# Expert layer of a two-layer decoder: slots inverted by one-hot products, rows gathered and results scattered inside the experts' stage, gate folded into a token-major projection

## The chip, the cores and the metric

One core of one Trainium2 chip runs the whole program. The metric is the device time of one execution in microseconds (us); lower is better. The core's engines are TensorE (PE), VectorE (DVE), ScalarE (ACT), GpSimd (POOL) and SyncE (SP), which here only issues DMAs. Each engine runs its own list of instructions in order and waits on semaphores; an instruction that waits holds up all that stand behind it on the same engine.

## The reference, cut to what matters

The program is two decoder layers on x of 2 x 1024 tokens by 256. The change is in the last block, a mixture of 8 experts of which each token takes 2:

```python
h = x @ W_in + b_in                       # x: after layernorm, 2048 x 256
t = h.reshape(B * S, -1)
logits = t @ W_gate + b_gate              # 2048 x 8
probs = jax.nn.softmax(logits, axis=-1)
topv, topi = jax.lax.top_k(probs, TOP_K)  # TOP_K = 2
topv = topv / jnp.sum(topv, axis=-1, keepdims=True)
route = jnp.zeros_like(probs).at[jnp.arange(t.shape[0])[:, None], topi].set(topv)
mid = jax.nn.relu(jnp.einsum('nd,edh->neh', t, W1) + b1)    # W1: 8 x 256 x 1024
eout = jnp.einsum('neh,ehd->ned', mid, W2) + b2             # W2: 8 x 1024 x 256
moe_out = jnp.einsum('ne,ned->nd', route, eout)
out = moe_out.reshape(B, S, -1) @ W_out + b_out             # added to x
```

## The kernel before, in words

`x` stays in SBUF as 16 blocks (`NT`) of 128 tokens (`P`). The expert layer is three programs one after the other, each ended by a barrier of all engines.

`moe_prepare`: LayerNorm in 4 groups of 4 blocks; PE transposes to `mp_xt`; the projection with W_in gives `mp_full` with the features on the partitions (L1827); the gate (`Route.tensor`, L919) multiplies `mp_full` by W_gate, 128x8 at a time; PE transposes `mp_full` back (L1839) and ACT copies it to `mp_token`. DVE picks two experts per token and `Places.vector` computes a slot number for each choice: the choices are sorted by expert, and each expert's list is padded to a multiple of 256 rows (`RT`). That makes 23 tiles (`TILES`) of 256 slots, each with one expert. POOL first fills `moe_rows` in DRAM with zeros through `mp_zeros` (L1806, L1796), and then scatters each block of tokens twice by indirect DMA, 32 in all (L1813).

`moe_experts`: a loop over the 23 tiles. SP loads the tile's 256 rows into `me_row` (2 buffers), its biases, and the expert's W1 and W2 in 4 chunks of 512 KB (`me_chunk`, 4 buffers). ACT and DVE split each chunk into a high and a low part (`me_w_parts`, L2023 and L2058), the rows likewise (`take`, `me_h`), so that each product is three fp32r products. PE's order is written out by hand: `first(u+1)`, then `turn(u+2)` (the transposition of the rows of tile u+2), then `second(u)`. `first` makes the 8 blocks of the middle layer (L1983), ACT and DVE turn each into `me_mid` (L2045, L2047, L2086), `second` makes the result (L1997), and DVE's `finish(u - 2)` adds b2 into `me_result` (L2075) after the fifth block of tile u:

```python
for u in range(TILES):
    for b in range(HB):
...
        if b == HB - 1 and u + 1 < TILES:
            take(u + 1)
...
        if b == 4 and u >= 2:
            finish(u - 2)
```

POOL stores each result tile as it lies (L1957).

`moe_collect`: for each block of 128 tokens POOL gathers the two result rows of each token by indirect DMA (L2135, 32 in all, 4 buffers); DVE scales and adds them (L2186, L2188), PE transposes (L2146) and multiplies by W_out (L2158), DVE adds to `x` (L2179). Then `x` is stored.

## Time and profile before

| | us |
|---|---|
| median of 3 runs | 1904.73 (1901.89 to 1906.77) |
| the profiled execution's own time | 1912.87 |
| its span | 1911.2 |
| PE busy in the span | 1438.0 (75%) |
| DVE busy | 1089.6 (57%) |
| ACT busy | 898.0 (47%) |
| POOL busy | 308.2 (16%) |

The span is the time from the first to the last instruction of the profiled execution; starts of instructions are counted from its beginning. Busy shares are averages over stages of different kinds. The expert layer begins at 1423.2 us.

### The profile page before, as it was taken

The page shows a single profiled execution, that of the slowest core. Times are in us where ns is not written, and L with a number is a line of the kernel's source. Part 1 is how long each engine was busy: PE and PEld are TensorE (multiplying, and loading weights), DVE is VectorE, ACT ScalarE, POOL GpSimd, SP SyncE. Part 2 cuts the span into 40 slices and gives each one's busy share as a digit, 9 for nine tenths or more (in the row PEclk, how much of TensorE's full clock was granted, in tenths as well). Part 3 has the DMA queues.
Part 4 walks back from the last instruction along what each step waited for, and adds up shares of the span by engine and source line. Part 5 has one row for each costly group of instructions (what it writes and reads, how often), then busy time and mean ns, then how long its engine had stood idle before and what let it go on. Part 6 is the DMA issues. An engine that isn't in the chain of part 4 may idle for free. (4 is left out here: it accounts for less than half of the span.)

```text
span 1911.2 us, 28538 instructions
## 1 busy us (share of the span) xinstructions
PE 1438.0 (75%) x10307; PEld 1073.4 (56%) x10307; DVE 1089.6 (57%) x2450; ACT 898.0 (47%) x2137; POOL 308.2 (16%) x338
## 2 busy tenths in 40 slices
PE   4758889988589999789981453588868059999964
PEld 2413333334379999656760231477755059999953
DVE  3657766741655555455668647456553047777753
ACT  1503555553256666331104775366542057887731
POOL 1200000002223333200001525100010600000034
PEclk8858999998799999979995665799887579999987
DMA  2371322200200000110000000211112256766623
GB/s 68 132 99 20 49 35 35 35 2 9 81 1 2 1 1 2 34 39 1 0 23 9 1 6 14 64 35 34 34 47 88 88 188 219 222 216 217 227 85 103
DMA packets 92688, 122.59 MB, mean 64 GB/s; under 512 B 22221, under 2 KB 74051, under 8 KB 92291
## 3 DMA queue, kind: packets, MB, share of 16 engines
q1 hardware_dynamic: 86675, 105.85, 20.5%
q0 software_dynamic: 4912, 14.42, 2.1%
q8 instruction: 83, 1.36, 0.3%
q10 hardware_dynamic: 960, 0.47, 0.1%
q14 instruction: 58, 0.48, 0.1%
HBM read 88.60 MB, written 24.67 MB: 59 GB/s over the span
## 5 line engine op out<-in xcount | busy, mean ns | idle before, releaser
L759 DVE TENSOR_REDUCE sa_top<-ps 128x1 f32<-128x512 f32 (+3 forms) x384 | 197.2, 553 | 96.3 <-PE ps L751 65.3
L787 ACT ACTIVATE sa_probs<-ps 128x1024 f32<-128x1024 f32 (+4 forms) x192 | 150.8, 811 | 204.1 <-PE ps L772 145.6
L751 PE MATMUL ps<-sa_k,sa_q 96*128 96x512 bf16 (+3 forms) x384 | 125.5, 365 | 55.5 <-DMA sa_k<-scr_k 28.5
L1983 PE MATMUL ps<-me_h,me_w_parts 128*128 128x256 f32 x1104 | 142.0, 289 | 14.5 <-DVE me_w_parts L2058 7.9
L1983 PEld LDWEIGHTS ps<-me_h,me_w_parts 128*128 128x128 f32 x1104 | 136.8, 192 | 18.7 <-issue 15.3
L1997 PE MATMUL ps<-me_w_parts,me_mid 128*128 128x256 f32 x1104 | 136.2, 283 | 6.1 <-DVE me_result L2075 6.1
L1997 PEld LDWEIGHTS ps<-me_w_parts,me_mid 128*128 128x128 f32 x1104 | 132.3, 188 | 10.5 <-issue 10.5
L2735 ACT ACTIVATE cx_p<-ps,cx_top 128x154 f32<-128x154 f32 x256 | 97.2, 389 | 86.4 <-DVE cx_top L2799 86.4
L751 PEld LDWEIGHTS ps<-sa_k,sa_q 96*128 96x128 bf16 x384 | 35.1, 98 | 160.7 <-DVE sa_top L759 89.1
L2058 DVE TENSOR_TENSOR me_w_parts<-me_chunk,me_w_parts 128x1024 fp32r<-128x1024 f32 x92 | 112.8, 1226 | 21.4 <-ACT me_w_parts L2023 18.6
L2045 ACT ACTIVATE me_full<-ps,me_b 128x256 f32<-128x256 f32 x184 | 95.0, 517 | 57.6 <-PE ps L1983 54.5
L2086 DVE TENSOR_TENSOR me_mid<-me_full,me_mid 128x256 fp32r<-128x256 f32 x184 | 76.9, 422 | 65.8 <-ACT me_mid L2047 65.8
L772 PE MATMUL ps<-sa_q,sa_k 99*128 99x512 bf16 (+3 forms) x384 | 108.2, 335 | 7.6 <-ACT sa_probs L787 7.5
L2023 ACT ACTIVATE me_w_parts<-me_chunk 128x1024 fp32r<-128x1024 f32 x92 | 104.6, 1137 | 3.8 <-DMA me_chunk<-in_L_ffn_W_dram 3.8
L3164 ACT ACTIVATE cn_p<-ps,cn_top 128x154 f32<-128x154 f32 x256 | 82.1, 397 | 43.7 <-DVE cn_top L3248 43.5
L2047 ACT ACTIVATE me_mid<-ps,me_b 128x256 fp32r<-128x256 f32 x184 | 96.2, 523 | 0.0
L2597 POOL TENSOR_TENSOR cx_pn<-cx_p,cx_rinv 128x512 f32<-128x512 f32 x64 | 66.8, 1043 | 171.3 <-DVE cx_rinv L2807 171.2
L1058 PE MATMUL ps<-f_w_high,f_hid 128*128 128x512 f32 (+1 forms) x320 | 91.9, 373 | 0.0
L796 PE MATMUL ps<-sa_probs,v_all 128*32 128x512 f32 (+3 forms) x768 | 76.9, 503 | 0.0
L850 POOL TENSOR_TENSOR x<-x,po_b 128x256 f32<-128x256 f32 x16 | 11.0, 727 | 361.8 <-DMA po_w<-in_L_attn_Wout_dram 361.8
L772 PEld LDWEIGHTS ps<-sa_q,sa_k 99*128 99x128 bf16 x384 | 38.0, 100 | 49.5 <-ACT sa_probs L787 16.9
L1957 POOL DMA_DIRECT2D moe_results<-me_result x23 | 16.6, 720 | 301.1 <-DVE me_result L2075 301.1
(397 smaller groups left out, 3530.7 us busy)
## 6 DMA issues: line engine op xcount, KB each, us to landing
me_chunk<-in_L_ffn_W_dram SPq DMA_DIRECT2D x92, 512.0 KB, 5.4
sa_q<-scr_q SPq DMA_DIRECT2D x48, 128.0 KB, 4.8
sa_k<-scr_k SPq DMA_DIRECT2D x48, 128.0 KB, 7.7
moe_rows<-mp_zeros SPq DMA_DIRECT2D x2, 2944.0 KB, 12.7
me_row<-moe_rows SPq DMA_DIRECT2D x23, 256.0 KB, 3.8
moe_results<-me_result POOLq DMA_DIRECT2D x23, 256.0 KB, 3.2
cn_qd<-cn_qh SPq DMA_DIRECT2D x64, 64.0 KB, 2.0
scr_q<-h_part SPq DMA_DIRECT2D x6, 512.0 KB, 3.9
```

The lines of the kernel that those rows point to most:

```text
L751: last = pe.matmul(c.ps[:, bank, 0:w], self.q_st[0:96, slot, h, P * sb:P * sb + P], self.k_st[0:96, slot, h, k0:k0 + w], start=True, stop= ...
L759: return dve.tensor_reduce(self.top2[:, k0 // 512, ST * h + sb:ST * h + sb + 1], self.c.ps[:, bank, 0:w], AX.X, ALU.max)
L772: last = pe.matmul(out[:, 0:qw], self.k_st[0:KROWS, slot, h, P * kb:P * kb + P], self.q_st[0:KROWS, slot, h, P * kb + q0:P * kb + q0 + qw] ...
L787: return act.activation(dst, src, ACT.Exp, scale=self.width ** -0.5)
L1058: last = pe.matmul(ps[:, 4 + n % 4, 0:w], hid[:, g % 2, net, m, part, cols], wt[:, m, w0:w0 + w], start=(i == 0), stop=(i == len(terms) - 1))
L1983: last = pe.matmul(ps[:, MID + n % 4, 0:RT], w[:, u % 2, 0, i, DM * k + P * b:DM * k + P * b + P], h[:, u % 2, j, k, :], start=(m == 0), s ...
L1997: last = pe.matmul(ps[:, OUT + n % 2, 0:D], mid[:, u % 2, b, i, P * a:P * a + P], w[:, u % 2, 1, j, D * b:D * b + D], start=(m == 0), stop ...
L2023: act.activation(part(n, 0), chunk[:, n % BUF, :], ACT.Copy).then_inc(w_high.sem, 1)
L2045: act.activation(full[:, n % 4, :], ps[:, MID + n % 4, 0:RT], ACT.Relu, bias=col).then_inc(s_full.sem, 1)
L2047: act.activation(mid[:, u % 2, b, 0, :], ps[:, MID + n % 4, 0:RT], ACT.Relu, bias=col).then_inc(high.sem, 1)
L2058: dve.tensor_tensor(part(n, 1), chunk[:, n % BUF, :], raw(part(n, 0)), ALU.subtract).then_inc(w_low.sem, 1)
L2735: last = act.activation(p[:, h + i, :], ps[:, S_BANK + n % SR, M * i:M * i + M], ACT.Exp, bias=top[:, t % 2, h + i:h + i + 1], accum_out=d ...
```

## The change

The three programs become two. `moe_prepare`, `Places` and the use of `Route` and `LayerNorm` go; a class `Prepare` runs at the head of `moe_experts` instead, without a barrier between it and the experts. In it:

- PE first forms W_in @ W_gate and sets it beside W_in (`WL` = 264 columns). The projection is then one product with the tokens on the partitions, whose last 8 columns are the logits. It starts while LayerNorm of later groups still runs, and ACT takes half of LayerNorm's blocks.
- The tokens are stored to DRAM in their own order (`moe_tokens`, 4 plain DMAs on SP); the zero fill and the 32 scatters go.
- The slot numbers are inverted: with a slot = 128 a + b, DVE builds one-hot rows of a (`one_a`) and of b (`one_b`), POOL multiplies one of them by the list number (`pool_scale`), and 32 PE products of 92 columns give for each slot which token stands there. From that DVE forms `source` (the row to read) and `target` (where the result goes).
- In the experts' loop POOL gathers a tile's rows by `source` (two indirect DMAs of 128 rows), scatters its results by `target` to where the tokens' two results lie in order (two more), and adds b_out to one block of `x` in each of the first 16 tiles. SP's loop loses the row load and orders the weights ahead of the biases.
- `moe_collect` loads all results with 8 plain DMAs of 512 KB, 4 on SP and 4 on ACT. ACT takes one of the two scalings from DVE. W_out and b_out are loaded at the start of `Prepare`.

The diff, cut to its core:

```diff
+        for m in range(KD):
+            last = pe.matmul(ps[:, 5, E8 * KD:E8 * KD + E8], self.b_cols[:, m, :], self.w_gate[:, m, :],
+                             start=(m == 0), stop=(m == KD - 1))
+        last.then_inc(self.s["gate_made"].sem, 1)
+        turn(1)
+        pe.wait_ge(self.s["gate_set"].sem, self.s["gate_set"].at(2))
+        for g in range(NG):
+            hidden(g)
+            if g + 2 < NG:
+                turn(g + 2)
...
+        for i in range(LISTS):
+            if i % 8 == 0:
+                pe.wait_ge(self.s["hot_b"].sem, self.s["hot_b"].at(i // 8 + 1))
+            if i == 0:
+                pe.wait_ge(self.s["scaled"].sem, self.s["scaled"].at(2))
+            last = pe.matmul(ps[:, self.LIST, 0:2 * SLOTS], self.one_b[:, i, :],
+                             self.named[:, i, :, :].rearrange("p a s -> p (a s)"), start=(i == 0), stop=(i == LISTS - 1))
+        last.then_inc(self.s["listed"].sem, 1)
...
+        reverse = self.rev[:, :].unsqueeze(1).to_broadcast([P, NT, E8])
+        for j, src in enumerate((logits, self.rest[:, :, :])):
+            then(dve.tensor_reduce(self.top[:, j, :], src, AX.X, ALU.max))
+            then(dve.tensor_tensor(self.same[:, :, :], src, spread(self.top[:, j, :]), ALU.is_equal))
+            then(dve.tensor_tensor(self.scored[:, :, :], self.same[:, :, :], reverse, ALU.mult))
+            then(dve.tensor_reduce(self.rank[:, j, :], self.scored[:, :, :], AX.X, ALU.max))
+            then(dve.tensor_tensor(self.pick[:, j, :, :], self.scored[:, :, :], spread(self.rank[:, j, :]), ALU.is_equal))
+            if j == 0:
+                then(dve.scalar_tensor_tensor(self.rest[:, :, :], self.pick[:, 0, :, :], FAR, logits, ALU.mult, ALU.add))
+        dve.tensor_tensor(self.gone[:, 0, :], self.top[:, 1, :], self.top[:, 0, :], ALU.subtract).then_inc(self.s["gap"].sem, 1)
...
+        dve.tensor_tensor(self.one_a[:, :, :], self.iota_a[:, :].unsqueeze(1).to_broadcast([P, LISTS, SLOTS]),
+                          self.slot_a[:, :].unsqueeze(2).to_broadcast([P, LISTS, SLOTS]), ALU.is_equal
+                          ).then_inc(self.s["hot_a"].sem, 1)
+        dve.wait_ge(self.s["hot_a"].sem, self.s["hot_a"].at(1))
+        dve.tensor_scalar(self.named[:, :, 0, :], self.one_a[:, :, :], self.col[:, :], None, ALU.mult
+                          ).then_inc(self.s["scaled"].sem, 1)
...
+        for q in range(LISTS // 8):
+            a = slice(8 * q, 8 * q + 8)
+            dve.tensor_tensor(self.one_b[:, a, :], self.iota_b[:, :].unsqueeze(1).to_broadcast([P, 8, P]),
+                              self.slot_b[:, a].unsqueeze(2).to_broadcast([P, 8, P]), ALU.is_equal
+                              ).then_inc(self.s["hot_b"].sem, 1)
+        dve.wait_ge(self.s["listed"].sem, self.s["listed"].at(1))
+        then(dve.tensor_copy(self.found[:, :, :].rearrange("p a s -> p (a s)"), ps[:, self.LIST, 0:2 * SLOTS]))
+        then(dve.scalar_tensor_tensor(self.value[:, :], self.found[:, 1, :], float(P), self.found[:, 0, :],
+                                      ALU.mult, ALU.add))
+        then(dve.tensor_scalar(self.late[:, :], self.value[:, :], N + 0.5, -float(N), ALU.is_ge, ALU.mult))
+        then(dve.scalar_tensor_tensor(self.late[:, :], self.late[:, :], -1.0, self.value[:, :], ALU.add, ALU.add))
+        dve.tensor_scalar(self.source[:, :], self.late[:, :], 0.0, None, ALU.max).then_inc(self.s["sourced"].sem, 1)
...
-                sp.wait_ge(zero.sem, zero.at(1))
-                for i in range(ZERO):
-                    sp.dma_start(rows[P * per * i:P * per * (i + 1), :].rearrange("(p r) d -> p (r d)", p=P),
-                                 zeros[:, :]).then_inc(zeroed.sem, 16)
-                sp.wait_ge(bset.sem, bset.at(1))
...
-                pool.memset(zeros[:, :], 0.0).then_inc(zero.sem, 1)
-                places.pool(pool)
-                pool.wait_ge(zeroed.sem, zeroed.at(16 * ZERO))
-                pool.wait_ge(places.placed.sem, places.placed.at(1))
-                for t in range(NT):
-                    pool.wait_ge(tset.sem, tset.at(t + 1))
-                    for j in range(TK):
-                        pool.indirect_dma_start(rows, bass.IndirectOffsetOnAxis(ap=place[:, t, j:j + 1], axis=0),
-                                                token[:, t, :], None).then_inc(sent.sem, 16)
-                pool.wait_ge(sent.sem, sent.at(16 * NT * TK))
...
-                route.tensor(pe, full, w_gate)
-                for t in range(NT):
-                    if t >= 8 and t % 2 == 0:
-                        pe.wait_ge(tset.sem, tset.at(t - 6))
-                    for k in range(KD):
-                        last = pe.transpose(ps[:, t // 2 % 4, D * (t % 2) + P * k:D * (t % 2) + P * k + P],
-                                            full[:, k, P * t:P * t + P], c.ident[:, :])
...
             def _(sp):
+                pr.sync_loads(sp, w_out, b_out)
+                pr.sync_stores(sp, tokens, b1_cols)
                 for u in range(TILES):
...
-                    if u >= 2:
-                        sp.wait_ge(turned.sem, turned.at(u - 1))
-                    sp.dma_start(row[:, u % 2, :, :], rows[RT * u:RT * u + RT, :].rearrange("(a p) d -> p a d", p=P)
-                                 ).then_inc(row_in[u % 2].sem, 16)
...
+                    e = sp.value_load(pr.expert[0:1, u:u + 1], min_val=0, max_val=E8 - 1)
+                    def weights(q):
...
+                    weights(0)
+                    weights(1)
...
+                def gather(u):
+                    if u >= 2:
+                        pool.wait_ge(turned.sem, turned.at(u - 1))
+                    for a in range(SUB):
+                        at = bass.IndirectOffsetOnAxis(ap=pr.source[:, SUB * u + a:SUB * u + a + 1], axis=0)
+                        pool.indirect_dma_start(row[:, u % 2, a, :], None, tokens, at).then_inc(row_in[u % 2].sem, 16)
+                def scatter(u):
+                    pool.wait_ge(added.sem, added.at(SUB * (u + 1)))
+                    for a in range(SUB):
+                        at = bass.IndirectOffsetOnAxis(ap=pr.target[:, SUB * u + a:SUB * u + a + 1], axis=0)
+                        pool.indirect_dma_start(results, at, result[:, u % 2, a, :], None).then_inc(stored[u % 2].sem, 16)
...
+                gather(0)
+                gather(1)
+                pool.wait_ge(pr.s["targeted"].sem, pr.s["targeted"].at(1))
                 for u in range(TILES):
-                    pool.wait_ge(added.sem, added.at(SUB * (u + 1)))
-                    pool.dma_start(results[RT * u:RT * u + RT, :].rearrange("(a p) d -> p a d", p=P),
-                                   result[:, u % 2, :, :]).then_inc(stored[u % 2].sem, 16)
+                    if u < NT:
+                        pool.tensor_tensor(c.x[:, u, :], c.x[:, u, :], b_out[:, :], ALU.add).then_inc(biased.sem, 1)
+                    if u + 2 < TILES:
+                        gather(u + 2)
+                    scatter(u)
+                pool.wait_ge(biased.sem, biased.at(NT))
                 for i in range(2):
-                    pool.wait_ge(stored[i].sem, stored[i].at(16 * len(range(i, TILES, 2))))
...
+        def load(eng, j):
+            for g in range(NG):
+                r0 = N * j + 4 * P * g
+                eng.dma_start(got[:, j, 4 * g:4 * g + 4, :],
+                              results[r0:r0 + 4 * P, :].rearrange("(t p) d -> p t d", p=P)).then_inc(got_in[j][g].sem, 16)
...
-                sp.dma_start(bb[:, :], c.arg["L1_ffn_b_out"].rearrange("(a b) -> a b", a=1).partition_broadcast(P)
-                             ).then_inc(w_in.sem, 16)
-                sp.dma_start(w[:, :, :], c.arg["L1_ffn_W_out"].rearrange("(k p) n -> p k n", p=P)
-                             ).then_inc(w_in.sem, 16)
...
-            def _(pool):
-                for t in range(NT):
-                    if t >= RING:
-                        pool.wait_ge(summed.sem, summed.at(t - RING + 1))
-                    for j in range(TK):
-                        pool.indirect_dma_start(got[:, t % RING, j, :], None, results,
-                                                bass.IndirectOffsetOnAxis(ap=place[:, t, j:j + 1], axis=0)
-                                                ).then_inc(got_in[t % RING].sem, 16)
+                load(sp, 0)
...
+                load(act, 1)
+                def weigh(t):
+                    act.wait_ge(got_in[0][t // 4].sem, got_in[0][t // 4].at(16))
+                    if t >= 2:
+                        act.wait_ge(summed.sem, summed.at(t - 1))
+                    act.activation(part[:, t % 2, :], got[:, 0, t, :], ACT.Copy, scale=share[:, 0, t:t + 1]
+                                   ).then_inc(weighed.sem, 1)
+                weigh(0)
+                weigh(1)
...
-                dve.wait_ge(w_in.sem, w_in.at(32))
-                for t in range(NT):
-                    dve.tensor_tensor(c.x[:, t, :], c.x[:, t, :], bb[:, :], ALU.add).then_inc(biased.sem, 1)
...
-                    dve.wait_ge(got_in[t % RING].sem, got_in[t % RING].at(16 * TK * (t // RING + 1)))
+                    dve.wait_ge(got_in[1][t // 4].sem, got_in[1][t // 4].at(16))
+                    dve.wait_ge(weighed.sem, weighed.at(t + 1))
                     if t >= 2:
                         dve.wait_ge(turned.sem, turned.at(t - 1))
-                    m, g = mixed[:, t % 2, :], got[:, t % RING, :, :]
-                    dve.tensor_scalar(m, g[:, 0, :], share[:, t, 0:1], None, ALU.mult).then_inc(weighed.sem, 1)
-                    dve.wait_ge(weighed.sem, weighed.at(t + 1))
-                    dve.scalar_tensor_tensor(m, g[:, 1, :], share[:, t, 1:2], m, ALU.mult, ALU.add
-                                             ).then_inc(summed.sem, 1)
+                    dve.scalar_tensor_tensor(mixed[:, t % 2, :], got[:, 1, t, :], share[:, 1, t:t + 1], part[:, t % 2, :],
+                                             ALU.mult, ALU.add).then_inc(summed.sem, 1)
```

POOL's instructions in the experts' loop, in the order before. `[waits signal49]` is here `added`, DVE's count of finished result halves.

```order
L1953 UNCONDITIONAL_BRANCH [waits barrier_Pool_Activation_PE_DVE_SP_gather]
L1957 DMA moe_results<-me_result 128x2x256 [waits signal49] x23
L1922 UNCONDITIONAL_BRANCH [waits me_stored1,me_stored0]
```

The same place after. `signal54` is `added`, `signal44` is `turned` (PE's count of transposed row tiles); the first four gathers are those of tiles 0 and 1.

```order
L2072 DMA me_row<-moe_tokens,mp_source 128x256 [waits signal31,signal21]
L2072 DMA me_row<-moe_tokens,mp_source 128x256 x3
L2088 TENSOR_TENSOR x<-x,moe_b_out 128x256 [waits signal32]
L2072 DMA me_row<-moe_tokens,mp_source 128x256 [waits signal44]
L2072 DMA me_row<-moe_tokens,mp_source 128x256
L2078 DMA moe_results<-me_result,mp_target 9984x256 [waits signal54]
L2078 DMA moe_results<-me_result,mp_target 9984x256
L2088 TENSOR_TENSOR x<-x,moe_b_out 128x256
L2072 DMA me_row<-moe_tokens,mp_source 128x256 [waits signal44]
L2072 DMA me_row<-moe_tokens,mp_source 128x256
L2078 DMA moe_results<-me_result,mp_target 9984x256 [waits signal54]
L2078 DMA moe_results<-me_result,mp_target 9984x256
```

A stage that was one plain DMA a tile is now an add, two gathers and two scatters; the gathers of tile 3 stand behind the scatters of tile 0, and so on.

PE after, from the last block of `first(2)` to `second(1)` and `first(3)`. `me_row_in1` is the landing of the gathers of tile 3.

```order
L2117 MATMUL ps<-me_h,me_w_parts 128x256 [waits signal51]
L2117 MATMUL ps<-me_h,me_w_parts 128x256 x5
L2104 MATMUL ps<-ident,me_row 128x128 [waits signal46,me_row_in1]
L2104 MATMUL ps<-ident,me_row 128x128 x3
L2131 MATMUL ps<-me_w_parts,me_mid 128x256 [waits signal54,signal52,signal48]
L2131 MATMUL ps<-me_w_parts,me_mid 128x256 x23
L2131 MATMUL ps<-me_w_parts,me_mid 128x256 [waits signal54]
L2131 MATMUL ps<-me_w_parts,me_mid 128x256 x23
L2117 MATMUL ps<-me_h,me_w_parts 128x256 [waits signal51,signal48,signal46]
L2117 MATMUL ps<-me_h,me_w_parts 128x256 x5
```

PE's order within the experts' loop is as before; what the transposition waits for has moved from SP's load to POOL's gathers.

## Rows read from the trace of the kernel before

**Rows 1.** Timeline, preparation: start us, duration us, engine, line, operation, count [idle before].

```profile
1423.17 5.01 POOL L1806 MEMSET mp_zeros<- 128x5888 f32 x1 [60.17 <-POOLq L2933]
...
1424.93 3.42 DVE L180 TENSOR_SCALAR lnm_ve<-lnm_mv 128x4 f32<-128x4 f32 x1
...
1441.22 13.95 PE L1827 MATMUL ps<-mp_xt,mp_w 128*128 128x512 f32 x32
...
1455.95 12.26 PE L919 MATMUL ps<-mp_gate,mp_full 128*128 128x8 f32 x64 [0.78 <-ACT mp_full L1851]
...
1468.24 0.29 DVE L933 TENSOR_TENSOR rt_logits<-ps,rt_bias 128x128 f32<-128x128 f32 x1 [26.59 <-PE ps L919]
...
1542.77 7.48 PE L1983 MATMUL ps<-me_h,me_w_parts 128*128 128x256 f32 x47 [7.93 <-DVE me_w_parts L2058]
```

**Rows 2.** Busy time by stretch: PE, PEld, DVE, ACT, POOL, granted clock, DMA share, GB/s.

```profile
1484.00:1531.00 47.00, 0.00 (x0) 0.00 (x0) 1.15 (x5) 0.00 (x0) 31.09 (x32) 0.50 0.22 89
...
1545.00:1830.00 285.00, 272.48 (x2192) 264.33 (x2190) 204.37 (x334) 230.49 (x475) 14.42 (x20) 0.99 0.65 209
...
1552.00:1556.00 4.00, 0.00 (x0) 0.00 (x0) 3.88 (x6) 3.58 (x7) 0.00 (x0) 0.66 0.63 212
...
1857.00:1903.00 46.00, 29.00 (x96) 20.21 (x96) 18.46 (x48) 6.14 (x16) 24.36 (x25) 0.70 0.26 75
```

**Rows 3.** Indirect DMAs by tile, time on POOL: min/median/max ns, first and last start.

```profile
L1813 POOL DMA_INDIRECT moe_rows<-mp_token,moe_place x32: 959/963/1244, 1485.0 to 1524.6; - x32
...
L2135 POOL DMA_INDIRECT mc_got<-moe_results,moe_place x32: 946/949/1170, 1848.1 to 1892.2; - x32
```

**Rows 4.** Timeline, one tile of the experts.

```profile
1810.79 6.06 PE L1983 MATMUL ps<-me_h,me_w_parts 128*128 128x256 f32 x48
1811.83 0.47 ACT L2045 ACTIVATE me_full<-ps,me_b 128x256 f32<-128x256 f32 x1 [2.40 <-PE ps L1983]
...
1816.68 0.60 PE L1970 MATMUL ps<-ident,me_row 128*128 128x128 f32 x4
...
1816.98 0.75 DVE L2075 TENSOR_TENSOR me_result<-ps,me_b 128x256 f32<-128x256 f32 x2
...
1817.55 5.93 PE L1997 MATMUL ps<-me_w_parts,me_mid 128*128 128x256 f32 x48 [0.27 <-DVE me_result L2075]
...
1818.03 0.72 POOL L1957 DMA_DIRECT2D moe_results<-me_result  x1 [11.91 <-DVE me_result L2075]
...
1822.09 1.23 DVE L2058 TENSOR_TENSOR me_w_parts<-me_chunk,me_w_parts 128x1024 fp32r<-128x1024 f32 x1
1823.42 6.05 PE L1983 MATMUL ps<-me_h,me_w_parts 128*128 128x256 f32 x48
```

**Rows 5.** Costliest groups: an add of 256 elements on POOL.

```profile
L850 POOL TENSOR_TENSOR x<-x,po_b 128x256 f32<-128x256 f32 x16 | 11.0, 727 | 361.8 <-DMA po_w<-in_L_attn_Wout_dram 361.8
```

**Rows 6.** DMA issues: count, KB each, median us from issue to landing.

```profile
me_chunk<-in_L_ffn_W_dram SPq DMA_DIRECT2D x92, 512.0 KB, 5.4
...
me_row<-moe_rows SPq DMA_DIRECT2D x23, 256.0 KB, 3.8
```

**Rows 7.** Timeline, collection.

```profile
1847.44 0.35 SPq L2124 DMA_DIRECT2D mc_b<-in_L_ffn_b_out_dram  x1
...
1873.37 0.42 DVE L2179 TENSOR_TENSOR x<-ps,x 128x256 f32<-128x256 f32 x1 [6.50 <-remote]
...
1884.22 0.95 POOL L2135 DMA_INDIRECT mc_got<-moe_results,moe_place  x1 [0.30 <-issue]
...
1887.67 0.34 DVE L2186 TENSOR_SCALAR mc_mixed<-mc_got,moe_share 128x256 f32<-128x256 f32 x1
...
1901.88 0.43 DVE L2179 TENSOR_TENSOR x<-ps,x 128x256 f32<-128x256 f32 x1 [1.01 <-PE ps L2158]
```

**Rows 8.** Timeline of PE alone, the second tile of the experts.

```profile
1556.93 7.37 PE L1983 MATMUL ps<-me_h,me_w_parts 128*128 128x256 f32 x48 [6.13 <-issue]
```

532 lines of the change are left out of this document (309 added, 223 removed).

## The prediction

> **What bounds the kernel now.** I read the table of stages first, then the timeline of each stage. The change touches only the last 488 us of the span, the second layer's expert part, and that part is four stretches with four different bounds.
>
> Preparation, 1423.2 to 1484. LayerNorm, projection, gate and a transposition follow each other. [rows 1] show the projection's matmuls at 13.95 us and then the gate's 64 at 12.26 us, with VectorE (DVE) idle until the logits are complete at 1468.24; the slot numbers are complete just before the first scatter at 1485.0 [rows 3]. At the front a 5.01 us memset on GpSimd (POOL) runs beside a DVE instruction on 4 values a partition that lasts 3.42 us, so DVE waits there.
>
> Scatter, 1484 to 1531. [rows 2] put no TensorE (PE) work at all there: POOL builds 32 indirect DMAs. Each is 0.96 us of POOL [rows 3], 1.27 us from start to start (1485.0 to 1524.6 over 31 steps). PE's first expert matmul comes at 1542.77 [rows 1].
>
> Experts, 1545 to 1830. PE is busy 272.5 of 285 us at a granted clock of 0.99 [rows 2]. One tile in [rows 4]: `first` starts at 1810.79 and at 1823.42, so a tile takes 12.63 us. Between them stand the transposition of the next rows (1816.68), which does not wait, and `second` (1817.55). DVE finishes the results of the tile two before at 1816.98 to 1817.73, and POOL sends them at 1818.03, after 11.91 us idle. POOL is idle nearly all the time, which decides nothing by itself.
>
> Collection, 1847.4 to 1902.3. 32 gathers at 0.95 us plus 0.30 us on POOL [rows 3] set the pace; PE is busy 29 of 46 us at clock 0.70 [rows 2].
>
> **The change part by part.** *Preparation and scatter.* The projection keeps its columns (32 matmuls of 264 in place of 16 of 512), but begins while LayerNorm runs, and brings the logits with it: 12.26 us of gate go. Eight loads instead of seven stand before PE, W_out among them, and two bias chains; I give back 2 us. So logits at about 1458. Then DVE's chain. From logits to the first scatter it took 16.8 us; now it has 11 operations for the two choices (0.32 each, by the 0.29 us row at 1468.24 and its gap), 1.3 for the counts, 1.2 through PE, 2.0 to `expert`, 3.0 to `slot_b`. The one-hot rows are new and have no row: `one_a` has 1472 elements and `one_b` four times 1024. The nearest row, a DVE operation on 1024 elements, takes 1.23 us [rows 4], so 1.8, 1.7 and 4.9 us; POOL's product of 1472 elements costs 4.2 us by its 0.73 us for 256 [rows 5] and lies beside them. With 1.9 for the last matmuls and the decoding it is 21 us: `source` at 1479. Two gathers (0.3 + 2.5), landing 2.5, transposition and two halves of `me_h` 2.6: first expert matmul at 1487 in place of 1542.77, **-56 us**. Weights load from `expert` (about 1466) on, beside all this. If the new broadcasts ran at half the element rate it is -45; if LayerNorm gains in full from the missing memset, -64.
>
> *Collection.* Eight plain loads of 512 KB on two queues replace the gathers. The nearest row, weights of 512 KB, lands in 5.4 us [rows 6], so the first product starts about 6 us after 1847.44. DVE loses 16 adds and 16 scalings. PE then has 1.8 us a token block at clock 0.70 (29.0/16), so about 1.3 at the full one: 3 blocks at 2.1 and 13 at 1.3, with a tail of 2, end 31 us after 1847.44 and not 54.9 [rows 7]: -24. But DVE stood 6.50 us there for a releaser that the trace does not know [rows 7], and such a stop would no longer hide behind POOL: I take **-20**, with -10 and -26 as bounds. The last tile's scatter is two indirect DMAs instead of one plain, **+2**.
>
> *Experts.* SyncE (SP) loses the row load, POOL gets two gathers, two scatters and one add a tile: 4 x 1.27 + 0.93, about 6.0 us of 12.6. By sum that fits. The order does not. POOL issues gather(u+3) behind scatter(u), and scatter(u) waits at POOL's head until `finish(u)` is done. DVE does `finish(u)` after the fifth `me_mid` of tile u+2, which needs `first(u+2)` on PE. And PE wants the rows of tile u+3 directly after `first(u+2)`. So gather(u+3) starts only when its rows are already due, for every u from 0 to 19: 20 tiles. The old row load on SP waited only for the transposition two tiles before. Behind PE's late transposition stand `second`, the next `first`, and ScalarE's (ACT) and DVE's `take`, then their splits.
>
> The period follows from [rows 4]. From the start of `first` to the end of `finish`: 1817.73 - 1810.79 = 6.94. ACT is idle 2.40 us before its first copy there, so it brings no backlog and this number stays. Then POOL: 0.30 to wake (1818.03 - 1817.73), two scatters 2.52, add 0.73 [rows 5] and 0.20, two gathers 2.20 up to the end of the second's building: 5.95. Landing has no row of its own. Above: a gather built at 1885.17 was read at 1887.67 at the latest, 2.5 [rows 7]; the plain row load took 3.8 beside the weights [rows 6]. Below I put 1.5 (that row load less its issue and queueing, an estimate). I take 2.5. Then the transposition and `second` up to the next `first`, 0.60 + 5.87. Sum 21.86. PE stands 9 us before that; after 6.13 us idle, in which the granted clock fell (0.66 on average over its end) [rows 2], 48 matmuls took 7.37 instead of 6.05 [rows 4, 8]: +1.4. Period **23.3**, 10.6 more than 12.63. The add is there in 15 of the 20 cases: 15 x 10.6 + 5 x 9.7 = **+208 us**. Lower bound, landing 1.5, no clock loss, no gap at the add: 8.0, in all +156. Upper, landing 3.8, four builds at 1.17 [rows 3], clock loss doubled: 14.3, in all +282.
>
> Sum: 208 - 56 - 20 + 2 = **+134 us**. The profiled execution took 1912.87 around a span of 1911.2, 8 us above the median 1904.73; all terms are differences, so I put them on the median: **2039 us** (2047 on the profiled one).
>
> **A page that bears on it.** In the trace, gathers took up to 1.17 us of POOL where 0.95 is the median [rows 3]. The Trainium skill, in "SBUF — State Buffer", section "SBUF: two separate sides", says of DMAs issued from GpSimd that their descriptors can't be written while DVE holds the shared port in a two-port mode, and gives 620 ns growing to 3100. The trace agrees in direction only, with a tenth or two in place of five times. What it would do here is the second rival.
>
> **The rivals.** *Faster, 7 in 100: the rows are not late.* If POOL's building overlapped its waits, or gathers cost it nothing, the tile would stay at 12.63 and the gains stay: 1904.7 - 74 = **1831**. For it: POOL idle 11.91 us a tile, and six more fit. Against: the order above, and indirect DMAs that follow each other at a fixed 1.27 us, never overlapping. It decides for faster from where finish-to-rows-landed takes under 16.3 - 6.94 - 6.47 = 2.9 us (74 us over 20 tiles allow 3.7 each); two scatters alone take 2.5.
>
> *Slower still, 8 in 100: the building waits for DVE.* If each of the four in the late chain waits for one of DVE's 1.23 us subtractions, 4.9 us a tile, +98: **2137**. For it the 1.17; against it that DVE stands at `take` when the gathers are built.
>
> *The clock, 3 in 100.* If pauses of 9 us keep PE at its lower level (1.2 GHz) through `second` and half of `first`, some 8 us a tile more: about **2180**. Against: 48 matmuls after 6.13 us idle lost only 1.3 us.
>
> *Preparation gains nothing, 4 in 100:* small operations and waits eat the gain of the gate and the scatter: 2039 + 56 less some, about **2085**.
>
> **How the numbers follow.** The forecast has 78 in 100. Its terms' bounds, all at once, give 1972 (156 - 64 - 26 + 1 = +67) and 2134 (282 - 45 - 10 + 2 = +229); the ends of all terms rarely meet, and with the rivals above it the range that leaves out 2 in 10 is 1985 to 2110. A change of 0.3% (about 6 us) is what a measurement of this kernel can tell from none. Slower: all but the first rival, 0.93. Within 0.3%: only if the late chain is close to 2.9 us, 0.01. Faster 0.06.
>
> **What would show it.** In the profile after: POOL's `me_row` gathers start within 5 us after DVE's `me_result`, and PE's transposition of `me_row` is preceded by 7 to 11 us idle in every tile from the fourth on, with the clock low after it; starts of `first` 21 to 25 us apart; experts about 500 us long in all; first expert matmul 50 to 60 us earlier; collection 25 to 35 us instead of 55. POOL busy share small all the same. Wrong would be: a tile period near 13 us, gathers that start before `me_result`, or a preparation as long as before.

## The result, and the profile after

The changed kernel takes 2066.0 us (median of 4 runs, 2065.5 to 2073.6) against 1904.5 us (4 runs, 1901.9 to 1906.8): ratio 1.086, 95% interval 1.083 to 1.088. The forecast was 2039 us in a range of 1985 to 2110. The profiled execution has a span of 2064.4 us; the one of before had 1911.2 us.

The page of the profile, two lines of its table of 40 slices (busy tenths of PE, and tenths of its granted clock). The experts fill slices 30 to 39. PE is at 5 and 6 there, once at 7, with the clock at 7 and 8; in the kernel before, whose line stands behind them, the experts' slices show 9:

```profile
PE   4569988876799997999246248886465566555574
...
PEclk9859999988899997899655569998787778887787
...
PE   4758889988589999789981453588868059999964
```

The chain of waits, 1500 to 1980 us (waiting line, releaser: us in total, times, longest):

```profile
POOL moe_results L2078 <- DVE me_result L2211: 355.7, 19, 34.4
...
PE ps L2104 <- DMA me_row<-moe_tokens,mp_source: 196.5, 19, 11.6
```

In the kernel before, PE's transposition of a tile's rows had no wait at all [rows 4]. Now it waits 10.3 us on average in each of the 19 tiles of this window, for the gather. One tile on the timeline of the changed kernel, to be read against [rows 4]:

```profile
1753.73 5.98 PE L2117 MATMUL ps<-me_h,me_w_parts 128*128 128x256 f32 x48
...
1759.86 0.75 DVE L2211 TENSOR_TENSOR me_result<-ps,me_b 128x256 f32<-128x256 f32 x2
...
1760.88 1.00 POOL L2078 DMA_INDIRECT moe_results<-me_result,mp_target  x1 [17.46 <-DVE me_result L2211]
...
1762.19 1.01 POOL L2078 DMA_INDIRECT moe_results<-me_result,mp_target  x1 [0.30 <-issue]
...
1762.79 1.58 DVE L2194 TENSOR_TENSOR me_w_parts<-me_chunk,me_w_parts 128x1024 fp32r<-128x1024 f32 x1
...
1763.22 1.73 POOL L2088 TENSOR_TENSOR x<-x,moe_b_out 128x256 f32<-128x256 f32 x1
...
1765.11 0.99 POOL L2072 DMA_INDIRECT me_row<-moe_tokens,mp_source  x1 [0.16 <-issue]
1766.40 0.96 POOL L2072 DMA_INDIRECT me_row<-moe_tokens,mp_source  x1 [0.30 <-issue]
1769.79 1.12 PE L2104 MATMUL ps<-ident,me_row 128*128 128x128 f32 x4 [10.08 <-DMA me_row<-moe_tokens,mp_source]
...
1770.56 7.23 PE L2131 MATMUL ps<-me_w_parts,me_mid 128*128 128x256 f32 x48
```

The reader is to follow one chain down the list: result finished at 1760.61, two scatters, addition, two gathers built by 1767.36, rows read at 1769.79, second product, and the next first product at 1777.62. PE's transposition and second product are slower than in [rows 4] and come later, and each step of this chain stands behind the one before it.

The stages, each read from the same points in both traces:

| stretch | before | after | difference |
|---|---|---|---|
| start of the expert layer to first expert matmul | 119.6 | 67.7 | -51.9 |
| first expert matmul to the end of the last second product | 299.1 | 531.0 | +232.0 |
| from there to the first load or gather of the collection | 5.6 | 12.5 | +6.9 |
| from there to the last addition of the collection | 54.9 | 26.5 | -28.4 |

The sum is +158.6 us. The profiled execution reached the expert layer 4.8 us earlier (1418.4 and not 1423.2), ahead of anything the change touches, and its tail was 0.7 us shorter; that leaves the 153.2 us between the spans.

The end of the preparation, to be read against [rows 1] and [rows 3]:

```profile
1467.58 3.00 POOL L1752 TENSOR_TENSOR mp_xt<-mp_one_a,mp_list 128x1472 bf16<-128x1472 bf16 x1 [46.48 <-DVE mp_one_a L1952]
...
1467.98 7.08 DVE L1960 TENSOR_TENSOR mp_xt<-mp_iota_b,mp_slot_b 128x1024 bf16<-128x1024 f32 x4
...
1478.03 1.21 POOL L2072 DMA_INDIRECT me_row<-moe_tokens,mp_source  x1 [7.45 <-DVE mp_source L1969]
...
1486.13 7.73 PE L2117 MATMUL ps<-me_h,me_w_parts 128*128 128x256 f32 x48 [1.41 <-DVE me_h L2199]
```

The end of the experts and the start of the collection, to be read against [rows 7]:

```profile
2017.22 0.42 DVE L2211 TENSOR_TENSOR me_result<-ps,me_b 128x256 f32<-128x256 f32 x1 [2.32 <-PE ps L2131]
...
2019.20 0.97 POOL L2078 DMA_INDIRECT moe_results<-me_result,mp_target  x1 [0.30 <-issue]
2029.66 2.29 SPq L2258 DMA_DIRECT2D mc_got<-moe_results  x4
```

Two things stand out that the prediction had not. The tile periods are not all alike: the first 15 take 23.9 us on average (1514.43 to 1873.30), the last five, which have no addition on POOL, 25.1 us (1873.30 to 1998.73) and not less. And from the last scatter to the first load 9.5 us pass in which no engine computes.

### The profile page after: what moved, and what is told of

Same layout as the page of the kernel before. It is cut to its first block and busy times, and to the rows that moved or that the text cites. A ratio compares the mean times of both kernels' runs of the same rounds, so it can differ in the third digit from the quotient of the medians.

```text
span 2064.4 us, 28469 instructions
## 1 busy us (share of the span) xinstructions
PE 1446.0 (70%) x10291; PEld 1094.0 (53%) x10291; DVE 1102.5 (53%) x2396; ACT 903.2 (44%) x2142; POOL 347.6 (17%) x366
## 5 line engine op out<-in xcount | busy, mean ns | idle before, releaser
L2104 PE MATMUL ps<-ident,me_row 128*128 128x128 f32 x92 | 24.6, 419 | 214.1 <-DMA me_row<-moe_tokens,mp_source 214.1
L2131 PE MATMUL ps<-me_w_parts,me_mid 128*128 128x256 f32 x1104 | 163.7, 317 | 0.9 <-DVE me_result L2211 0.9
L2131 PEld LDWEIGHTS ps<-me_w_parts,me_mid 128*128 128x128 f32 x1104 | 160.5, 225 | 1.0 <-issue 1.0
L2223 DVE TENSOR_TENSOR me_mid<-me_full,me_mid 128x256 fp32r<-128x256 f32 x184 | 84.6, 464 | 141.4 <-ACT me_mid L2183 141.4
L2104 PEld LDWEIGHTS ps<-ident,me_row 128*128 128x128 f32 x92 | 15.9, 210 | 218.4 <-DMA me_row<-moe_tokens,mp_source 218.4
L2194 DVE TENSOR_TENSOR me_w_parts<-me_chunk,me_w_parts 128x1024 fp32r<-128x1024 f32 x92 | 117.6, 1279 | 22.5 <-ACT me_w_parts L2158 19.9
L2078 POOL DMA_INDIRECT moe_results<-me_result,mp_target x46 | 46.6, 1013 | 410.0 <-DVE me_result L2211 403.0
L2199 DVE TENSOR_TENSOR me_h<-ps,me_h 128x512 fp32r<-128x512 f32 x23 | 15.9, 691 | 140.9 <-ACT me_h L2164 140.9
```

What stands on the lines that cost most here:

```text
L2131: last = pe.matmul(ps[:, OUT + n % 2, 0:D], mid[:, u % 2, b, i, P * a:P * a + P], w[:, u % 2, 1, j, D * b:D * b + D], start=(m == 0), stop ...
L2194: dve.tensor_tensor(part(n, 1), chunk[:, n % BUF, :], raw(part(n, 0)), ALU.subtract).then_inc(w_low.sem, 1)
```

## The experiments

The theory: gather(u+3) stands on POOL behind scatter(u), which waits for a result that exists only when the rows of u+3 are due. The rivals: indirect transfers are slow in themselves; POOL and DVE disturb each other; PE's clock. All times below are medians; the kernel before was timed beside each, at 1905.8 to 1908.1 us, and the ratios are to it.

### The gather ahead of the wait

```diff
+                gather(2)
                 for u in range(TILES):
+                    if u + 3 < TILES:
+                        gather(u + 3)
                     if u < NT: pool.tensor_tensor(...)
-                    if u + 2 < TILES:
-                        gather(u + 2)
                     scatter(u)
```

> Edit: on POOL the row gather of tile u+3 is issued ahead of the addition and of the wait for tile u's result, instead of behind the scatters of tile u; nothing else differs from the changed kernel. Theory (the rows arrive late because the gathers stand behind the scatter's wait for the result): the rows are there when TensorE asks, a tile takes about 12.6 to 13.5 us again instead of 24.2, 20 tiles give back 20 x (24.2 - 13) = 224 us, and 2066 - 224 = about 1840 us. Rival A (the indirect transfers themselves are too slow beside the weight loads, whatever their place): the wait for the rows stays, the period stays at 22 us or more, 2020 us or more. Rival B (POOL's and VectorE's collisions take over as the bound): a period of 15 to 18 us, 1880 to 1940 us.

Measured: 1837.9 us, ratio 0.963 (0.960 to 0.966). The transfers and the additions are the same, the gathers stand elsewhere in POOL's list, and the kernel takes 228 us less than the changed one. Two neighbouring tiles on its timeline:

```profile
1604.72 6.04 PE L2118 MATMUL ps<-me_h,me_w_parts 128*128 128x256 f32 x48
...
1610.98 0.66 PE L2105 MATMUL ps<-ident,me_row 128*128 128x128 f32 x4 [0.22 <-DMA me_row<-moe_tokens,mp_source]
1611.47 5.94 PE L2132 MATMUL ps<-me_w_parts,me_mid 128*128 128x256 f32 x48
1611.94 1.01 POOL L2078 DMA_INDIRECT moe_results<-me_result,mp_target  x1 [5.71 <-DVE me_result L2212]
...
1614.55 1.37 POOL L2072 DMA_INDIRECT me_row<-moe_tokens,mp_source  x1 [0.30 <-issue]
...
1616.00 1.23 DVE L2195 TENSOR_TENSOR me_w_parts<-me_chunk,me_w_parts 128x1024 fp32r<-128x1024 f32 x1
1616.23 1.84 POOL L2072 DMA_INDIRECT me_row<-moe_tokens,mp_source  x1 [0.31 <-issue]
1617.33 6.05 PE L2118 MATMUL ps<-me_h,me_w_parts 128*128 128x256 f32 x48
```

The period is 12.61 us, that of before; the transposition waits 0.22 us. Over 20 tiles it is 12.65 against 24.21 on average: 231 us. Rivals A and B fall. Rival B's collisions are there: a gather takes 1.37 and 1.84 us of POOL instead of 0.96 (mean over the 46: 1.49), but POOL still idles 5.7 us a tile and the period does not grow.

### The order alone, in the kernel before

```diff
-                    sp.dma_start(row[:, u % 2, :, :], rows[...])       # SyncE, ahead of the weights
+                    if u + 2 < TILES:                                  # POOL, behind the store of u - 1
+                        load(u + 2)
```

> Edit of the kernel before: the plain load of a tile's rows moves from SyncE's queue to POOL's, where it stands behind the store of the tile's result, in the order of the changed kernel; no indirect transfer is added to it. Theory (the order on POOL's queue makes the stall): the period goes from 12.63 us to about 20 us (first product to result 6.9, store issue, landing of 4 to 5 us, transposition and second product 6.5), 20 x 7.5 = +150 us, about 2055 us. Rival (the indirect transfers make it, the order alone costs nothing): within 15 us of 1905 us.

Here `load(0)` and `load(1)` stand ahead of the loop, and `load(u + 2)` at its head, so that it follows the store of u - 1 as the gather does. Measured: 2057.6 us, +150 us, ratio 1.080 (1.075 to 1.085). One tile:

```profile
1956.19 0.75 DVE L2079 TENSOR_TENSOR me_result<-ps,me_b 128x256 f32<-128x256 f32 x2
1957.23 0.72 POOL L1961 DMA_DIRECT2D moe_results<-me_result  x1 [18.91 <-DVE me_result L2079]
1957.95 0.71 POOL L1953 DMA_DIRECT2D me_row<-moe_rows  x1
1962.25 1.12 PE L1974 MATMUL ps<-ident,me_row 128*128 128x128 f32 x4 [6.22 <-DMA me_row<-moe_rows]
1963.02 7.90 PE L2001 MATMUL ps<-me_w_parts,me_mid 128*128 128x256 f32 x48
```

With no scatter, no gather and no addition in the stage, the period is 20.1 us. So the order alone costs 7.5 of the 11.6 us that a tile lost. The other 4.1 are a difference of two kernels, not the price of one thing: in the two tiles shown, POOL needs 6.8 us from the result to the second gather where it needs 1.7 here to the end of the load's issue, and the rows land 2.4 us behind that where they take 3.6 here.

### The addition out of the chain

```diff
-                    if u < NT: pool.tensor_tensor(...)
                     if u + 2 < TILES:
                         gather(u + 2)
+                    if u < NT: pool.tensor_tensor(...)
                     scatter(u)
```

> Edit: on POOL the bias addition of a tile stands behind the two gathers instead of ahead of them, all 16 additions stay. Theory (the addition, 1.73 us, and the gap of 0.2 us behind it lie on the late chain of result, scatters, addition, gathers, rows, transpositions, second product, result): 1.9 us less in each of 15 tiles, -28 us, about 2038 us. Rival (the arrival of the rows is set by the weight loads that are under way, as in the last five tiles, where the gathers were built 1.2 us earlier and the rows landed 2.8 us later): the rows land no earlier, 2060 to 2100 us.

Measured: 2065.8 us, ratio 1.083 (1.079 to 1.086). No change; the rival that the rows land no earlier stands, and the step of my working that priced this addition at its own duration falls. On its timeline:

```profile
1760.22 1.01 POOL L2078 DMA_INDIRECT moe_results<-me_result,mp_target  x1 [17.70 <-DVE me_result L2211]
...
1762.84 1.37 POOL L2072 DMA_INDIRECT me_row<-moe_tokens,mp_source  x1 [0.30 <-issue]
...
1764.51 0.97 POOL L2072 DMA_INDIRECT me_row<-moe_tokens,mp_source  x1 [0.30 <-issue]
1765.48 0.75 POOL L2090 TENSOR_TENSOR x<-x,moe_b_out 128x256 f32<-128x256 f32 x1
1769.24 1.11 PE L2104 MATMUL ps<-ident,me_row 128*128 128x128 f32 x4 [10.19 <-DMA me_row<-moe_tokens,mp_source]
```

The result was finished at 1759.94. From there the gathers are built in 5.5 us instead of 6.8, but the rows are read after 9.3 us in the one and 9.2 in the other: they land 3.8 us behind the gathers, not 2.4. Of the addition's 1.9 us, 0.4 went into a longer first gather and the rest into the transfer.

The run says something of the last five tiles too. Here POOL's chain from result to gathers is the same in all twenty tiles, yet the last five take 25.1 us each (1872.58 to 1998.05) and the fifteen before them 23.9, as in the changed kernel. So the longer period of the last five does not come from the missing addition. What it comes from no run shows.

### What holds the rows up in the transfer

Two kernels, both edits of the last one.

```diff
+                        if n >= BUF:           # half of every weight load, q < 2; likewise for q >= 2
+                            src, dst = src[:, 0:DM // 2], dst[:, 0:DM // 2]
                         sp.dma_start(dst, src).then_inc(w_in[n % BUF].sem, 16)
```

> Edit of e2_add_behind: from the second expert tile on each of the four weight loads of a tile fetches half of its bytes (256 KB instead of 512 KB; the other half of the buffer keeps old weights, so the outputs are not the reference's); every instruction on the engines stays. Theory (the rows' transfer takes 3.8 us behind the second gather instead of 2.4 because the weight loads keep the DMA engines at 70 to 90% while it runs): the rows land about 2.4 us behind the second gather, 1.4 us less in each of 20 tiles and a little more where the first gather shrinks from 1.37 to 1.0 us, -28 to -36 us, about 2034 us. Rival (the rows wait for the scatters that stand ahead of them in POOL's queue, 6.7 us from the second scatter's end to the transposition in both orders): within 8 us of 2066 us.

```diff
                 def scatter(u):
                     pool.wait_ge(added.sem, added.at(SUB * (u + 1)))
+                    if u + 3 < TILES:
+                        gather(u + 3)
                     for a in range(SUB): ...
```

> Edit of e2_add_behind: POOL still waits for tile u's result, but then issues the two gathers of tile u+3 first and the two scatters of tile u behind them. Theory (what makes a tile late is the whole chain from result to rows, of which the two scatters' 2.6 us of issue are a part, and the transfer then meets the weight loads wherever it is): the gathers are built 2.6 us earlier, of which some is lost again in the transfer, as the addition's 1.9 us was; the period falls by 0.5 to 2.6 us, -10 to -52 us, 2015 to 2055 us. Rival (the rows are held up by the scatters' transfers ahead of them in the queue): the rows land 2.4 us behind the second gather, 6.3 us after the result instead of 9.3, the period falls by 3 us or more, 2005 us or less. Rival (the weight loads set the arrival alone): no change, 2066 us.

Measured: 2050.9 us (1.077, 1.073 to 1.081) with half the weight bytes, and 2006.4 us (1.052, 1.049 to 1.055) with the gathers ahead of the scatters. A tile of the first:

```profile
1758.38 0.96 POOL L2077 DMA_INDIRECT me_row<-moe_tokens,mp_source  x1 [0.30 <-issue]
...
1761.82 1.11 PE L2109 MATMUL ps<-ident,me_row 128*128 128x128 f32 x4 [8.89 <-DMA me_row<-moe_tokens,mp_source]
```

Its second product, at 1762.58, takes 7.96 us. The rows land 2.5 us behind the second gather (1759.34 to 1761.82; 2.9 in the next tile) instead of 3.8, as the theory said, while the period falls only from 24.21 to 23.37 us. The wait shrinks by 1.2 us, from 10.2 (194.2 us in 19 times) to 9.1 (181.3 in 20), and the second product grows by 0.3, from 7.2 to 7.5 on average (172.1 us over 23 tiles against 166.0). So weight traffic delays the rows by about 1.3 us a tile; the total missed the expected range (-15 us against -28 to -36), since the first gather did not shrink (1.37 us, as before) and the second product gave some back.

And a tile of the second:

```profile
1769.20 0.98 POOL L2072 DMA_INDIRECT me_row<-moe_tokens,mp_source  x1 [16.44 <-DVE me_result L2212]
1770.49 1.01 POOL L2072 DMA_INDIRECT me_row<-moe_tokens,mp_source  x1 [0.30 <-issue]
1771.80 1.41 POOL L2080 DMA_INDIRECT moe_results<-me_result,mp_target  x1 [0.30 <-issue]
...
1775.01 1.11 PE L2105 MATMUL ps<-ident,me_row 128*128 128x128 f32 x4 [6.99 <-DMA me_row<-moe_tokens,mp_source]
```

The period is 21.19 us, 3.0 less than 24.21: more than the scatters' 2.6 us of issue. The total lies below the range of the theory (2015 to 2055 us) and within 2 us of what the first rival had, by which the scatters' own transfers hold the rows up (2005 us or less). Its figure for the rows, 6.3 us behind the result, is nearly met as well (6.1: 1768.93 to 1775.01). Its other figure is not: the rows land 3.5 us behind the second gather here and 4.6 in the tile before, not 2.4. So that rival is neither confirmed nor excluded; the second one, by which the weights set the arrival alone, had no change and falls. What is shown: 2.6 us earlier in the queue brought 3.0 us a tile, 1.9 us earlier brought nothing, and weight traffic takes part. Why the one gain came through and the other did not stays open, since no run here moved the weight loads in time alone.

### TensorE's clock

```diff
                 def turn(u):
-                    pe.wait_ge(row_in[u % 2].sem, ...)
                     if u >= 2:
                         pe.wait_ge(h_low.sem, h_low.at(u - 1))
+                    if u >= 3:
+                        for _ in range(21):
+                            pe.matmul(ps[:, TURN[u % 2], 0:WL], c.ident[:, :], pr.w[:, 0, :], start=True, stop=True)
+                    pe.wait_ge(row_in[u % 2].sem, ...)
```

> Edit: ahead of the wait for a tile's rows TensorE runs 21 products of no use (identity by a 264-column constant, into the bank that the transposition then overwrites), about 9 us of work in a wait of 10 us; they keep the granted clock up and leave the outputs alone. Theory (1.2 to 1.9 us of the period is TensorE's clock falling in the wait: second product 7.23 us instead of 5.93, transposition 1.12 instead of 0.60): -1.7 x 20 = -34 us, about 2032 us. Rival (the second product is slow for another reason than the idle time ahead of it, or the filler delays the transposition by what it wins): within 10 us of 2066 us, or slower.

Measured: 2039.4 us, -26.7 us, ratio 1.069 (1.066 to 1.073).

```profile
1757.13 0.66 PE L2107 MATMUL ps<-ident,me_row 128*128 128x128 f32 x4 [0.48 <-DMA me_row<-moe_tokens,mp_source]
1757.55 5.94 PE L2134 MATMUL ps<-me_w_parts,me_mid 128*128 128x256 f32 x48
```

With PE busy ahead of them, transposition and second product take 0.66 and 5.94 us, as in [rows 4]; in the changed kernel they took 1.12 and 7.23. Windows over the tile of the changed kernel show its clock (us, busy PE, PEld, DVE, ACT, POOL; PEclk, DMA share, GB/s): 0.67 over the wait, 0.58 over the first 4 us of work behind it, then full. From 1753 to 1777 us the changed kernel has 0.79 and the one with the filler products 1.00.

```profile
1760.00:1769.00 9.00, 0.00 (x0) 0.00 (x0) 4.93 (x7) 3.49 (x7) 5.70 (x5) 0.67 0.72 233
1770.00:1774.00 4.00, 4.00 (x22) 4.00 (x22) 1.92 (x2) 1.55 (x2) 0.00 (x0) 0.58 0.00 0
1774.00:1778.00 4.00, 4.00 (x36) 4.00 (x35) 0.00 (x0) 0.00 (x0) 0.00 (x0) 1.00 0.54 167
```

0.58 is near the lower of the engine's two levels, 1.2 of 2.4 GHz, which would be 0.5. The period falls by 1.6 us (22.59), 33 us over 20 tiles; the run gained 27. The profiled executions say where part of the rest lies: this one reached the expert layer 3.7 us later (1422.1 and not 1418.4), ahead of anything that was edited, and from there to the end of the span it is 31 us shorter.

### The end of the experts' stage

> Edit of e1_gather_first: three small fills of an unused tile on POOL, one behind the last scatter, ahead of the wait for the scatters, and one behind each of the two waits. In e1 the last packet of the scatters is moved at 1791.9 us, and the first load of the collection is issued at 1800.5 us, 8.6 us later, with no packet on any queue between. Reading A (the arrival of the scatters' signal is late): the last mark stands at 1799 us or later on e1's clock. Reading B (the signal comes 1 to 2 us behind the packets, and the time goes in the end of the stage on POOL): the last mark stands at about 1794 us and the collection still starts at about 1800.5 us. Time in both: within 3 us of e1's 1837.9 us.

Measured: 1837.3 us (0.964, 0.961 to 0.967), so the marks cost nothing.

```profile
1790.95 0.13 POOL L2095 MEMSET me_mark<- 128x8 f32 x1
1792.44 0.14 POOL L2098 MEMSET me_mark<- 128x8 f32 x2 [1.36 <-DMA moe_results<-me_result,mp_target]
1800.59 2.75 SPq L2263 DMA_DIRECT2D mc_got<-moe_results  x4
```

Reading B: the scatters have landed 1.5 us behind their issue; 8.0 us go between POOL's last instruction of the stage and the first of the next. Three edits of the kernel before ask what it depends on.

```diff
                     pool.dma_start(results[...], result[:, u % 2, :, :]).then_inc(stored[u % 2].sem, 16)
+                    if u == 0:            # one gather; second kernel: u == TILES - 1; third: two at each u < 20, with waits for their buffers
+                        pool.indirect_dma_start(extra[:, :], None, rows, ...).then_inc(extra_in.sem, 16)
```

> Edit of the kernel before: one needless gather of 128 rows into an unused tile, on POOL behind the first tile's store, 280 us ahead of the stage's end. Theory (indirect transfers in a stage make POOL's part of the stage's end longer, whenever they were issued): from the end of the last second product to the collection's first load about 12 us instead of 5.6, 1911 us. Rival (what counts is the number of transfers on POOL's queue, or that they stand last): 5.6 to 6.5 us, within 2 us of 1905 us.

> Edit of the kernel before: the one needless gather of e9_before_one_gather stands behind the last tile's store instead of behind the first's. Theory (what lengthens POOL's end of the stage is that an indirect transfer is the last thing issued on its queue): from the end of the last second product to the collection's first load 10 us or more instead of 5.3 to 5.6, 1910 us. Rival (what counts is how many indirect transfers the stage issued, or nothing of them): 5.5 us and the 1.3 us of the gather's own issue, 1906 us.

> Edit of the kernel before: two needless gathers behind the store of each of the first twenty tiles (40 in all), none near the end, beside a path that does not wait for POOL. Theory (the number of indirect transfers lengthens POOL's end of the stage): from the end of the last second product to the collection's first load about 12 us, as with the 92 of the changed kernel, 1911 us. Rival (the number does not count): 5.5 us, within 3 us of 1905 us. In both the tiles' period stays at 12.6 us, since nothing waits for these gathers; a period over 12.9 us would say that 2.5 us of descriptor building a tile already disturb the other engines.

Measured: 1906.4 us (1.000, 0.999 to 1.002), 1906.5 us (0.999, 0.997 to 1.001) and 1909.1 us (1.001, 0.999 to 1.003); the total tells none of them from no change, so the verdicts rest on the traces. In the third, where no gather is near the end:

```profile
1836.76 0.42 DVE L2084 TENSOR_TENSOR me_result<-ps,me_b 128x256 f32<-128x256 f32 x1 [2.32 <-PE ps L2006]
1837.49 0.72 POOL L1958 DMA_DIRECT2D moe_results<-me_result  x1 [4.95 <-DVE me_result L2084]
1845.78 0.35 SPq L2135 DMA_DIRECT2D mc_b<-in_L_ffn_b_out_dram  x1
```

From the end of the last `me_result` to the next stage's first issue, with the number of transfers that POOL issued in the stage:

| kernel | transfers on POOL | us | less a second issue behind the last result |
|---|---|---|---|
| before | 23 | 5.2 | 5.2 |
| one gather, early | 24 | 5.3 | 5.3 |
| one gather, last | 24 | 6.7 | 5.3 |
| rows on POOL (plain loads and stores only) | 46 | 7.1 | 7.1 |
| forty gathers | 63 | 8.6 | 8.6 |
| after; gather first | 92 | 12.0 | 10.7 |

It grows by about 0.08 us for each transfer, plain or indirect, and one gather costs the same at the start and at the end of the stage. The preparation of the kernel before, with 32 scatters on POOL, fits too: there 5.4 us lie between the last issue and the next stage (1525.58 to 1530.93), with 23 transfers 4.2 (1843.27 to 1847.44) and with 46 it is 6.0 (1990.53 to 1996.57). Of what these kernels vary, the number of transfers is what the time follows; POOL's waits, which mostly come with the transfers, were not varied alone. The theory of the first of the three kernels and that of the second fall; the third's holds in direction (8.6 us for 63, not 12). Beside the forty gathers the tiles' period stayed at 12.64 us (1704.67 to 1717.31): building them lengthens no path of the tile there.

### The collection's loads ahead of that end

```diff
+                for i in range(2):                       # SyncE, behind its last weight load; ScalarE likewise with load(act, 1)
+                    sp.wait_ge(stored[i].sem, stored[i].at(16 * SUB * len(range(i, TILES, 2))))
+                load(sp, 0)
```

> Edit of e1_gather_first: the eight loads of the scattered results are issued within the experts' stage, by SyncE and ScalarE as soon as the scatters' signals have come, into the half of the weight parts that the last tile does not use; the collection's stage then begins with the results on their way. Theory (in e7 the scatters' signals were there at 1792.4 us and the collection's first load went out at 1800.6 us, 8.2 us of stage end with no transfer; the first results landed 5.0 us after their issue): the loads run inside the stage's end, the 5.0 us are saved, about 1833 us against e1's 1838. Rival (the stage's end itself is the wait for the transfers' queues and gets longer by what is issued ahead of it): no gain, 1838 us.

> The kernel of e1_gather_first again, unchanged, beside e8_collect_loads_early on the same chip, so that the two can be compared over five rounds: 1837.9 us within 0.3%.

Measured: 1835.5 us (0.963, 0.961 to 0.965) against 1835.5 us of the unchanged one (0.965, 0.962 to 0.968). In the profile the edit does what it was to do:

```profile
1790.75 0.42 DVE L2226 TENSOR_TENSOR me_result<-ps,me_b 128x256 f32<-128x256 f32 x1 [2.32 <-PE ps L2143]
...
1795.12 2.25 SPq L1662 DMA_DIRECT2D me_w_parts<-moe_results  x4
...
1803.18 0.91 ACT L2296 ACTIVATE mc_part<-me_w_parts,moe_share 128x256 f32<-128x256 f32 x2 [22.13 <-PEq L2040]
```

From the last result to the collection's first operation it is 12.0 us, and 17.0 in the kernel run beside it (1784.48 to 1801.52). The totals don't show these 5 us: the ratios differ by 0.2%, which their intervals cover. By the totals the edit is inconclusive. The traces say more. The execution with the early loads reached the expert layer at 1420.5 us, the one beside it at 1414.8, and nothing of that is the edit's; over all profiled executions of this case that point lies between 1414.8 and 1423.2. Counted from there to the end of the span, the three profiled executions of the gather-first order take 417.4, 417.5 and 416.9 us (the second with its marks) and the one with the early loads 413.6. So some 3 to 4 of the 5 us are gained in that one execution; whether it is so in every one is not shown.

## Why the prediction was right

**The mechanism held, point by point.** The gathers start 4.5 us behind `me_result`, the transposition waits 10 us in every tile from the fourth on, the fix by order alone removes it, and the order alone in the kernel before brings 7.5 of its 11.6 us a tile. The rival that the rows are not late had 1831 us, which is within 7 us of what the reordered kernel takes: its premise was wrong, and its sum of gains, 74 us, came out at 70 in that kernel's profile from layer start to last addition. The single terms were off by 5 (preparation), 8 (collection), 5 (stage's end) and 2 us (experts) and cancel, so that closeness is in part luck.

**The period.** Term by term, forecast and the tile shown above: first product to result 6.94 and 6.88; POOL 5.95 and 6.75; landing 2.5 and 2.43; transposition and second product with the clock's loss 7.87 and 7.83. Sum forecast 23.3 (rounded from 23.26), measured 23.89. By the terms the 0.6 us stand in POOL's part, where the addition is: I took its 0.73 us from a row where DVE was idle [rows 5]; here it took 1.73, and the DVE subtraction beside it 1.58 instead of 1.23. With the addition moved behind the gathers both are back at 0.75 and 1.23, but the period stays as it was. So the step "15 x 10.6 + 5 x 9.7", by which a tile without the addition is 0.9 us shorter, was wrong: taken out of the chain, the addition was worth nothing. A sum of terms one behind the other holds less strictly here than its closeness suggests, since the landing changes with the moment of the issue. The Trainium skill, in "SBUF — State Buffer", section "SBUF: two separate sides", says that a GpSimd operation that reads SBUF and a DVE operation with two SBUF inputs exclude each other from a shared port for a whole instruction. The trace agrees that both are longer (1.73 and 1.58 us); that the subtraction, which had started 0.4 us ahead (1762.79 and 1763.22), was longer too does not follow from the page's rule, by which the one that starts first has the port for its whole instruction.

**The experts: +232 against +208.** The 24 us missing are 10 from the first fifteen late tiles (11.3 us over the old period and not 10.6) and 14 from the last five: I gave them 9.7 us each over the old period for want of an addition, and they took 12.5 (25.09 - 12.63). Two steps failed there. One is the price of the addition, which was worth nothing. The other is "landing 2.5" as one value: rows of such a tile landed 5.2 us behind the gather (1909.51 to 1914.72). The half-weight kernel shows part of the cause, traffic of the weight loads; why the last five are longer than the rest stays open.

**The clock.** +1.4 us a tile was forecast; the filler products gave 1.6 back. The rival that put it at 8 us falls.

**Descriptor building held up by DVE** (the rival at 2137 us): in the late chain the gathers took 0.99 and 0.96 us, so it did not act there. Where gathers run beside DVE's subtractions, in the reordered kernel, they took up to 1.84 us: the direction was as the rival had it, the price 0.4 to 0.9 us a gather and not 1.2, and it was hidden. The rows show when it acts. A building that began ahead of a subtraction took its usual time (the scatter at 1611.94 took 1.01 us, with a subtraction from 1612.17 on). One that began under a subtraction took longer by about what was left of it: 0.41 us with 0.52 left (the gather at 1614.55), 0.88 with 1.00 left (1616.23), and likewise a scatter in the kernel with the gathers ahead of the scatters (1771.80: 1.41 us, with 0.54 left).

**Preparation: -51.9 against -56.** The first gather starts 59.6 us into the layer (1478.03 from 1418.40); forecast 56.1 (1479.3 from 1423.2). The logits were 1.3 us later than I had them (36.1 and not 34.8). The four parts of `one_b` took 7.08 us where I had 4.9: PE's matmuls behind them start 1.13 us apart, so three took 1.13 each and the first, beside POOL's product of 3.00 us, 3.7. I had put that product beside DVE's work at no cost. No run took the product away, so that it made the first quarter long is read from this one overlap.

**Collection: -28.4 against -20.** The stop of 6.50 us for an unknown releaser [rows 7], for which I kept 4 us as a cost, did not come back. That is half of the 8.4 us. The other half is the pace: the last additions of the collection stand 1.11 us apart (2041.60 to 2051.59 in nine steps) where I had 1.3 us a block, and the tail is shorter than the 2 us I gave it. The value without the stop, -24 to -26, was the better reading.

**The stage's end: +6.9 against +2.** "Two indirect DMAs instead of one plain" was the wrong thing to count: 69 more transfers on POOL's queue in the whole stage are 5.5 us by the table above, and the second scatter 1.3. What POOL does in that time stays open.

The sum of the terms is 158.6 against 134; the errors of the experts and the stage's end (+29) and those of preparation and collection (-4) add up to the 25 us, and the median of 2066 lies 27 above the forecast.

## What to carry to other kernels

When a load moves to a queue that also holds a wait for a result, ask which instruction stands ahead of it at the moment when it should start: an engine that idles 11.9 of 12.6 us can still be late by a whole round trip. Lay out the queue so that loads for later tiles stand ahead of the wait for the present one; here that order was worth 228 us and turned a loss of 8.6% into a gain of 3.7%. And shortening a chain that ends in a transfer need not pay: 1.9 us taken out ahead of the gather were given back in its landing, though 2.6 us taken out brought 3.0. When a small gain is looked for late in a kernel, count it from the stage's own start: here that start moved by up to 8 us between executions.
